# Second cross-attention of a two-layer decoder: row normalisation on ScalarE, its shift on GpSimd, statistics and aggregates as two steps, second key group turned earlier

## The chip, the cores and the metric

The kernel runs on one core of a Trainium2 chip, as a single launch that computes the whole decoder. The metric is the device time of that launch in microseconds. Before the change it is 2525.32 us, the median of 3 runs (2520.55 to 2530.87).

## The reference

A post-norm decoder of two layers on x (32 sequences of 100 rows, 256 wide) with a context of 32 times 361 rows, 256 wide. Each layer is attention, cross-attention and a feed-forward part, each followed by a layer norm of its input plus its output. The change lies in the cross-attention of the second layer, for each of the 32 sequences:

```python
q_in  = layernorm(x, gamma, beta)             # 100 x 256
kv_in = layernorm(ctx, gamma, beta)           # 361 x 256
q, k, v = q_in @ Wq.T, kv_in @ Wk.T, kv_in @ Wv.T   # 16 heads of 16
q, k = rope(q), rope(k)
attn = softmax(q @ k.T * 16 ** -0.5 + temporal_bias)
a    = (attn @ v) @ Wout.T + b_out
gate = sigmoid(a @ Wgate.T + b_gate)
out  = gate * a + (1 - gate) * x
x    = layernorm(x + out)                     # no gamma, beta
```

Everything is float32 here.

## The kernel before, in words

`decoder` calls seven stages, one behind the other: self attention, strided cross-attention, routing, experts, linear attention, `cross_attention` (the stage of this case, program names beginning with `xa_`) and the last feed-forward part (`bf_`). The linear attention (`la_`) before it also normalises rows, with ScalarE doing the product (L2145) and GpSimd computing a negated mean, the root and their product (L1939, L1944, L1947).

`cross_attention` handles one sequence ("batch" b) per period; NB is 32. Each engine runs its own program: a function `body(b, has)` is called once for each b, and `periods` calls it for all b, with a loop for the middle ones. Within one body an engine works on up to five sequences at once, at offsets -2 to +4; `later(b, 2)` is the sequence two ahead. The order of the calls in `body` is the order of the engine's instructions, written out by hand, and an engine never goes past an instruction that waits. The waits are on semaphores: `at(b, per, nth)` is the count that a semaphore has once the nth of `per` signals for b is given.

The 361 context rows of a sequence are cut into three chunks of 121 rows that share their border rows; with the 100 rows of x, padded, as a fourth lot, they fill `rows_t[121, 2, 4, 256]` (two buffers, by the parity of b). The steps for one sequence, with the engine:

1. SyncE loads the four lots (`rows`, L2492 and L2494), once the rows that were in that buffer are normalised.
2. VectorE: `moments` (four row statistics L2893, four aggregates L2898, variance plus epsilon L2902). GpSimd: `raise_power`, the power -0.5 of 121x4 numbers (L2845). VectorE: `normalise`, four times (rows - mean) * root, 121x256 each (L2909).
3. TensorE: `turn_rows`, eight transposes into the banks C1 and C2. ScalarE: `rows_out` applies gamma and beta (L2746).
4. TensorE projects keys and queries (`keys_first`, `keys_last_and_queries`) into C0 and C1. VectorE: `rope`, products with the cosine and sine tables (L2920), in two halves. GpSimd: `finish_rope`, their difference and sum (L2839, L2840).
5. TensorE: `turn_kq` for the four head groups j, each into bank C[j % 2] (L2594). ScalarE: `kq_out` copies each to `kqT` (L2786). Group 2 waits for the copy of group 0, which frees its bank, and group 3 for that of group 1.
6. TensorE: `score` for each group, 100 x 361 for four heads, into the four banks of A (L2609). VectorE: `maxima`, the row maxima of those 100 x 1444 (L2929). There is one A only: the scores, the transposed scores and their readers follow each other in it.
7. TensorE: `turn_queries` (L2621) takes the maxima along as one more column, `score_turned` for each of the three chunks computes scores the other way round, less the maxima (L2636). ScalarE: `exponential` (L2757). The product with the exponential of the bias is GpSimd's for chunks 0 and 1 (`apply_bias`, L2828) and VectorE's for chunk 2 (L2936).
8. TensorE: values (`values_first`, `values_last`), `attend` for each chunk (L2653), `turn_out`, `turn_y`, `project_out`. ScalarE copies between these (`oT` is L2752, once per sequence).
9. VectorE: `divide`, `differ` (L2954, waits for `project_out`), then ScalarE `gate` (tanh, L2780), VectorE `mix`, GpSimd `raise_power_out`, VectorE `finish` (L2975), SyncE `store`.

In TensorE's body the end runs: `values_last`, `turn_kq` 0, `score` 3, `attend` 1, `turn_kq` 1 to 3; the next body begins with `score` 0, `turn_queries`, `turn_rows`, `attend` 2, `score_turned` 0. In VectorE's: `maxima` 0, `mix`, `rope` 0, `maxima` 1, `divide`, `rope` 1, `moments`, `finish`, `maxima` 2, `normalise`, `differ`, `maxima` 3, `apply_bias`. In ScalarE's: queries, rows, `oT`, exponentials 0 and 1, values, `y_out`, exponential 2, values, `kq_out` 0, `gate`, `kq_out` 1 to 3. In GpSimd's: root of the output, bias product 0, `finish_rope`, `raise_power`, bias product 1, residual.

Of the kernel before, what the change touches and what calls it, by code (L numbers as in the profile page):

```python
# [2387 lines left out]
def cross_attention(nc, NB, x_in, x_out, w, src_len, held):  # L2388
# [9 lines left out]
    with held.ctx:  # L2398
# [42 lines left out]
        rstd = s.sb("rstd", [ROWS, LOTS])  # L2441
        power = s.sb("power", [ROWS, LOTS])
# [15 lines left out]
        stats_ready, mv_ready, var_ready, rstd_ready, normed = (s.sem(n) for n in ("stats_ready", "mv_ready", "var_ready", "rstd_ready", "normed"))  # L2458
# [21 lines left out]
        with nc.Block() as block:  # L2480
# [41 lines left out]
            def _(pe):  # L2522
# [157 lines left out]
                def body(b, has):  # L2680
# [36 lines left out]
                    if has(1):  # L2717
                        score(later(b, 1), 3, has(0))
                    if has(0):
                        attend(b, 1)  # L2720
                    if has(2):
                        for j in range(1, G):
                            turn_kq(later(b, 2), j)
# [4 lines left out]
            def _(act):  # L2728
                for sem, per in ((rowsT_ready, KC), (kqT_ready, G), (q2_ready, 1), (exp_ready, NCH), (v_ready, 2), (oT_ready, 1), (yT_ready, 1),
                                 (th_ready, 1)):  # L2730
                    act.sem_inc(sem, per * LEAD)
# [17 lines left out]
                def attended_out(b):  # L2749
                    act.wait_ge(av_done, at(b, NCH, NCH))  # L2750
                    act.wait_ge(y_turned, at(later(b, -1), 1, 1))
                    nc.scalar.activation(oT[:].rearrange("p g t -> p (g t)"), CA[:, 0:G * T], ACT.Copy).then_inc(oT_ready, 1)  # L2752

# [34 lines left out]
                def body(b, has):  # L2788
                    if has(0):
                        queries_out(b)  # L2790
                    if has(2):
                        rows_out(later(b, 2))
                    if has(-1):
                        attended_out(later(b, -1))
                    if has(0):
                        exponential(b, 0)
                        exponential(b, 1)
                    if has(1):
                        values_first(later(b, 1))
                    if has(-1):  # L2800
                        y_out(later(b, -1))
                    if has(0):
                        exponential(b, 2)
                    if has(1):
                        values_last(later(b, 1))
                    if has(2):
                        kq_out(later(b, 2), 0)
                    if has(-1):
                        gate(later(b, -1))
                    if has(2):  # L2810
                        for j in range(1, G):
                            kq_out(later(b, 2), j)

                periods(act, NB, FIRST, LAST, REACH, body)

            @block.gpsimd
            def _(pool):
                for sem, per in ((rstd_ready, 1), (summed, 1), (biased, NCH - 1), (less_ready, 1), (o_rstd_ready, 1)):
                    pool.sem_inc(sem, per * LEAD)
                nc.gpsimd.memset(power[:], -0.5).then_inc(power_set, 1)  # L2820
# [21 lines left out]
                def raise_power(b):  # L2842
                    pool.wait_ge(var_ready, at(b, 1, 1))
                    pool.wait_ge(normed, at(later(b, -1), 1, 1))
                    nc.gpsimd.tensor_tensor(rstd[:], var[:], power[:], ALU.pow).then_inc(rstd_ready, 1)  # L2845

# [12 lines left out]
                def body(b, has):  # L2859
                    if has(-2):  # L2860
                        raise_power_out(later(b, -2))
                    if has(0):
                        apply_bias(b, 0)
                    if has(2):
                        finish_rope(later(b, 2))
                    if has(3):
                        raise_power(later(b, 3))
# [9 lines left out]
            def _(dve):  # L2877
                for sem, per in ((stats_ready, 1), (mv_ready, 1), (var_ready, 1), (normed, 1), (roped, 2), (max_ready, G), (last_biased, 1),
# [10 lines left out]
                def moments(b):  # L2889
# [4 lines left out]
                    last.then_inc(stats_ready, 1)  # L2894
                    dve.wait_ge(stats_ready, at(b, 1, 1))
                    nc.vector.memset(spare[:], 0.0)
# [4 lines left out]
                    dve.wait_ge(rstd_ready, at(later(b, -1), 1, 1))  # L2901
                    nc.vector.tensor_scalar(var[:], mv[:, :, 1], LN_EPS, None, ALU.add).then_inc(var_ready, 1)  # L2902

                def normalise(b):
                    k = b[1] % 2
                    dve.wait_ge(rstd_ready, at(b, 1, 1))
                    dve.wait_ge(turned, at(later(b, -2), KC, KC))
                    for n in range(LOTS):
                        last = nc.vector.tensor_scalar(rows_n[:, k, n, :], rows_t[:, k, n, :], mv[:, n, 0:1], rstd[:, n:n + 1],  # L2909
                                                       ALU.subtract, ALU.mult)  # L2910
                    last.then_inc(normed, 1)
# [65 lines left out]
                def body(b, has):  # L2977
                    if has(1):
                        maxima(later(b, 1), 0)
                    if has(-2):  # L2980
                        mix(later(b, -2))
                    if has(2):
                        rope(later(b, 2), 0)
                    if has(1):
                        maxima(later(b, 1), 1)
                    if has(-1):
# [3 lines left out]
                    if has(3):  # L2990
                        moments(later(b, 3))
# [4 lines left out]
                    if has(3):  # L2996
                        normalise(later(b, 3))
# [7 lines left out]
                moments((0, 0))  # L3005
                dve.wait_ge(fused, 1)
# [5 lines left out]
                normalise((0, 0))  # L3012
# [567 lines left out]
```

## Time and profile before

| | |
|---|---|
| median of 3 runs | 2525.32 us (2520.55 to 2530.87) |
| the profiled execution, its own time | 2539.31 us |
| its span, first to last instruction | 2537.5 us |
| granted TensorE clock, mean of the span | 0.887 |
| TensorE busy (matmul) | 2118.6 us, 83% |
| VectorE | 1530.8 us, 60% |
| ScalarE | 950.6 us, 37% |
| GpSimd | 928.1 us, 37% |

The profile describes one execution, not the median one. Busy times are sums over the whole span, in which the seven stages follow each other; this stage fills about 1557 to 2344 us of it. PE is TensorE, PEld its weight loads, DVE VectorE, ACT ScalarE, POOL GpSimd and SP SyncE; "L2757" is a line of the kernel. In brackets behind a row of a timeline stands how long the engine was idle before it and what ended that. Busy time of TensorE is modelled and includes pipelining, so neighbouring rows overlap by some hundredths of a microsecond.

### The profile page before, as it was taken

How to read it: one execution, taken by the hardware profiler on the slowest of the kernel's cores; microseconds unless marked ns; L12 is line 12 of the kernel's file. 1: busy time of each engine (PE TensorE's matmuls, PEld its weight loads, DVE VectorE, ACT ScalarE, POOL GpSimd, SP SyncE). 2: the span in 40 equal slices, each digit the busy share in tenths (PEclk: the TensorE clock that was granted, in tenths of full speed). 3: DMA queues.
4: the chain of work that ended last, by engine and by line, in shares of the span. 5: the costliest groups of instructions: out<-in, count | busy, mean ns of one | idle time of the engine just before them, and what ended most of it. 6: DMA issues, size and time to landing. Idle time of an engine off the chain costs nothing. (4 is left out here: it accounts for less than half of the span.)

```text
span 2537.5 us, 58466 instructions
## 1 busy us (share of the span) xinstructions
PE 2118.6 (83%) x20310; PEld 1583.7 (62%) x20310; DVE 1530.8 (60%) x3550; ACT 950.6 (37%) x1881; POOL 928.1 (37%) x913
## 2 busy tenths in 40 slices
PE   6999997999776664788489996999999999996575
PEld 4666665777676554566388884666666666664233
DVE  1444443555454546233255455799999999984898
ACT  1444442333210110233134342344444444442897
POOL 0111111111134555223355431455555555553343
PEclk9999998999887786899789897899999999997555
DMA  6000003555311110877233311011110101000111
GB/s 208 30 29 29 29 25 130 207 205 212 133 48 35 34 33 23 259 222 221 73 100 90 98 44 46 21 32 31 32 32 23 32 31 32 30 13 9 52 58 46
DMA packets 157643, 192.74 MB, mean 76 GB/s; under 512 B 28517, under 2 KB 141160, under 8 KB 157559
## 3 DMA queue, kind: packets, MB, share of 16 engines
q1 hardware_dynamic: 147287, 189.03, 23.7%
q0 software_dynamic: 10272, 2.62, 0.5%
q8 instruction: 49, 0.80, 0.1%
q14 instruction: 35, 0.29, 0.0%
HBM read 140.74 MB, written 77.51 MB: 86 GB/s over the span
## 5 line engine op out<-in xcount | busy, mean ns | idle before, releaser
L2757 ACT ACTIVATE xa_prob<-xa_A 121x1600 f32<-121x1600 f32 x96 | 144.5, 1505 | 304.1 <-PE xa_A L2636 304.1
L2828 POOL TENSOR_TENSOR xa_prob<-xa_prob,xa_exp_bias 121x1600 f32<-121x1600 f32 x64 | 228.7, 3573 | 41.0 <-ACT xa_prob L2757 40.9
L2929 DVE TENSOR_REDUCE xa_kq<-xa_A 100x4 f32<-100x1444 f32 x128 | 211.6, 1653 | 21.3 <-PE xa_A L2609 21.1
L1409 POOL DMA_INDIRECT slot_rows<-rt_x_again,rt_slot_u x150 | 152.6, 1017 | 166.0 <-DVE rt_x_again L1527 103.5
L2909 DVE TENSOR_SCALAR xa_rows_n<-xa_rows_t,xa_mv,xa_rstd 121x256 f32<-121x256 f32 x128 | 142.4, 1172 | 1.1 <-POOL xa_rstd L2845 1.1
L2636 PEld LDWEIGHTS xa_A<-xa_q2T,xa_kqT 17*121 17x121 f32 x3072 | 93.9, 185 | 56.5 <-DVE xa_kq L2929 35.9
L696 DVE TENSOR_REDUCE sa_kq<-sa_A 100x16 f32<-100x1600 f32 x32 | 58.4, 1826 | 106.1 <-PE sa_A L457 106.1
L2609 PE MATMUL xa_A<-xa_kqT 16*100 16x361 f32 x1024 | 112.9, 510 | 9.9 <-ACT xa_prob L2757 6.8
L2636 PE MATMUL xa_A<-xa_q2T,xa_kqT 17*121 17x100 f32 x3072 | 109.3, 280 | 13.8 <-DVE xa_kq L2929 13.2
L1655 POOL DMA_INDIRECT contrib<-ex_y,ex_place_u x64 | 62.3, 973 | 158.5 <-ACT ex_y L1707 140.4
L2850 POOL TENSOR_TENSOR xa_o_rstd<-xa_o_var,xa_power 100x1 f32<-100x1 f32 x32 | 17.9, 560 | 252.1 <-DVE xa_o_var L2969 252.1
L1330 PEld LDWEIGHTS rt_H<-rt_xT,rt_ws 128*88 128x88 f32 x800 | 106.0, 179 | 3.7 <-issue 1.7
L654 POOL TENSOR_TENSOR sa_kq<-sa_rot_c,sa_rot_s 100x128 f32<-100x128 f32 x32 | 16.6, 519 | 247.3 <-DVE sa_rot_s L689 247.3
L2553 PE MATMUL xa_C<-xa_wk,xa_rows_T 128*121 128x256 f32 x384 | 105.4, 414 | 1.7 <-ACT xa_rows_T L2746 1.7
L1330 PE MATMUL rt_H<-rt_xT,rt_ws 128*88 128x128 f32 x800 | 106.6, 299 | 0.0
L1676 PE MATMUL ex_B<-ex_w,ex_xT 128*128 128x352 f32 x256 | 92.9, 524 | 14.8 <-issue 12.5
L1085 POOL TENSOR_TENSOR xs_rstd<-xs_var,xs_power 100x1 f32<-100x1 f32 x32 | 17.6, 550 | 232.1 <-DVE xs_var L1153 232.1
L2553 PE MATMUL xa_C<-xa_wv,xa_rows_T 128*121 128x256 f32 x384 | 101.3, 401 | 0.0
L906 PE MATMUL xs_K<-xs_ctxT,xs_wk 128*128 128x368 f32 x256 | 88.8, 490 | 10.7 <-DVE xs_y L1161 10.7
L2653 PEld LDWEIGHTS xa_CA<-xa_prob,xa_v 120*32 120x32 f32 (+1 forms) x3072 | 66.2, 111 | 43.5 <-issue 30.7
L2653 PE MATMUL xa_CA<-xa_prob,xa_v 120*32 120x100 f32 (+1 forms) x3072 | 87.8, 256 | 5.0 <-DVE xa_prob L2936 3.8
L2594 PE MATMUL xa_C<-xa_ident,xa_kq 121*128 121x121 f32 x512 | 74.1, 279 | 20.6 <-ACT xa_kqT L2786 16.3
(350 smaller groups left out, 5397.0 us busy)
## 6 DMA issues: line engine op xcount, KB each, us to landing
ex_w<-in_w13T SPq DMA_DIRECT2D x64, 352.0 KB
contrib<-xs_zero SPq DMA_DIRECT2D x30, 640.0 KB
la_rows<-contrib SPq DMA_DIRECT2D x16, 1200.0 KB
xs_ctxT<-in_ctxT SPq DMA_DIRECT2D x32, 512.0 KB
xa_rows_t<-in_ctx SPq DMA_DIRECT2D x96, 121.0 KB
ex_w<-in_w2T SPq DMA_DIRECT2D x64, 176.0 KB
slot_rows<-xs_zero SPq DMA_DIRECT2D x32, 272.0 KB
ex_x_t<-slot_rows SPq DMA_DIRECT2D x64, 136.0 KB, 2.2
```

What stands on the lines that cost most here:

```text
L906: last = nc.tensor.matmul(K[g][:, 0:NH * KPH], wk[:, c, g * P:(g + 1) * P], ctxT[:, k, c, :, 0:KPH], start=(c == 0), stop=(c == KC - 1))
L1330: last = nc.tensor.matmul(bank[:HC, m * P:(m + 1) * P], ws[:, c, m * HC:(m + 1) * HC], xT[:, k, c, :], start=(c == 0), stop=(c == KC - 1))
L1409: nc.gpsimd.indirect_dma_start(slot_rows, bass.IndirectOffsetOnAxis(slot_u[:, k, n:n + 1], 0), x_again[:, k, :], None, bounds_check=SLOTS ...
L1676: last = nc.tensor.matmul(B[u][:, 0:2 * FE], xT[:, u, c, :], w13[:, u, c], start=(c == 0), stop=(c == KC - 1))
L2553: last = nc.tensor.matmul(bank[:ROWS, o:o + D], rows_T[:, k, c, a:a + ROWS], wm[:, c, :], start=(c == 0), stop=(c == KC - 1))
L2609: last = nc.tensor.matmul(A[:T, h, 0:src_len], kqT[rows, k, j, src_len:src_len + T], kqT[rows, k, j, 0:src_len], start=True, stop=True)
L2636: last = nc.tensor.matmul(A[:ROWS, h, j * T:(j + 1) * T], kqT[rows, k, j, n * STEP:n * STEP + ROWS], q2T[rows, j, :], start=True, stop=True)
L2653: last = nc.tensor.matmul(CA[32 * h:32 * h + 32, j * T:(j + 1) * T], v1[0:rows, k, n, 4 * j + h, :], prob[0:rows, n, o:o + T], start=(n == ...
L2757: nc.scalar.activation(prob[:, n, :].rearrange("p (h a) -> p h a", h=HPG), A[:ROWS, :, 0:G * T], ACT.Exp, scale=EXP_SCALE).then_inc(exp_re ...
L2828: nc.gpsimd.tensor_tensor(chunk, chunk, exp_bias[:, n, :].unsqueeze(1).to_broadcast([ROWS, HEADS, T]), ALU.mult).then_inc(biased, 1)
L2909: last = nc.vector.tensor_scalar(rows_n[:, k, n, :], rows_t[:, k, n, :], mv[:, n, 0:1], rstd[:, n:n + 1], ALU.subtract, ALU.mult)
L2929: nc.vector.tensor_reduce(kq[:T, k, NCH, 4 * j:4 * j + 4, DH:DH + 1].rearrange("p h o -> p (h o)"), A[:T, :, 0:src_len], axis=AXIS_X, op=A ...
```

## The change

The normalisation of the rows moves from VectorE to ScalarE, as root * row + shift, an activation with a scale and a bias from tiles; the shift, minus mean times root, is made by GpSimd with two small operations around the root (`nmean`, `shift`; `nothing` holds zeros). `moments` is split: the row statistics stand before `rope` 0 in VectorE's body, and `aggregate` stands between `maxima` 1 and `divide`. `raise_power` stands before `finish_rope` in GpSimd's body. `normalise` stands between `y_out` and exponential 2 in ScalarE's. `turn_kq` 1 stands before `attend` 1 in TensorE's.

```diff
--- before.py
+++ after.py
@@ -2439,6 +2439,9 @@
         mv = s.sb("mv", [ROWS, LOTS, 2])
         var = s.sb("var", [ROWS, LOTS])
         rstd = s.sb("rstd", [ROWS, LOTS])
+        nmean = s.sb("nmean", [ROWS, LOTS])
+        shift = s.sb("shift", [ROWS, LOTS])
+        nothing = s.sb("nothing", [ROWS, LOTS])
         power = s.sb("power", [ROWS, LOTS])
         o_stats = s.sb("o_stats", [T, 6])
         o_mv = s.sb("o_mv", [T, 2])
@@ -2455,7 +2458,8 @@
         loaded = [s.sem(f"loaded{k}") for k in range(2)]
         res_loaded = [s.sem(f"res_loaded{k}") for k in range(2)]
         stored = [s.sem(f"stored{k}") for k in range(2)]
-        stats_ready, mv_ready, var_ready, rstd_ready, normed = (s.sem(n) for n in ("stats_ready", "mv_ready", "var_ready", "rstd_ready", "normed"))
+        stats_ready, mv_ready, var_ready, rstd_ready, shift_ready, normed = (s.sem(n) for n in (
+            "stats_ready", "mv_ready", "var_ready", "rstd_ready", "shift_ready", "normed"))
         turned, rowsT_ready = s.sem("turned"), s.sem("rowsT_ready")
         projected, roped, summed = s.sem("projected"), s.sem("roped"), s.sem("summed")
         kq_turned, kqT_ready = s.sem("kq_turned"), s.sem("kqT_ready")
@@ -2716,10 +2720,12 @@
                         turn_kq(later(b, 2), 0)
                     if has(1):
                         score(later(b, 1), 3, has(0))
+                    if has(2):
+                        turn_kq(later(b, 2), 1)
                     if has(0):
                         attend(b, 1)
                     if has(2):
-                        for j in range(1, G):
+                        for j in range(2, G):
                             turn_kq(later(b, 2), j)
 
                 periods(pe, NB, FIRST, LAST, REACH, body)
@@ -2727,7 +2733,7 @@
             @block.scalar
             def _(act):
                 for sem, per in ((rowsT_ready, KC), (kqT_ready, G), (q2_ready, 1), (exp_ready, NCH), (v_ready, 2), (oT_ready, 1), (yT_ready, 1),
-                                 (th_ready, 1)):
+                                 (th_ready, 1), (normed, 1)):
                     act.sem_inc(sem, per * LEAD)
                 act.wait_ge(w_in, W_ALL)
                 act.wait_ge(cleared, 2)
@@ -2750,6 +2756,15 @@
                     act.wait_ge(av_done, at(b, NCH, NCH))
                     act.wait_ge(y_turned, at(later(b, -1), 1, 1))
                     nc.scalar.activation(oT[:].rearrange("p g t -> p (g t)"), CA[:, 0:G * T], ACT.Copy).then_inc(oT_ready, 1)
+
+                def normalise(b):
+                    k = b[1] % 2
+                    act.wait_ge(shift_ready, at(b, 1, 1))
+                    act.wait_ge(turned, at(later(b, -2), KC, KC))
+                    for n in range(LOTS):
+                        last = nc.scalar.activation(rows_n[:, k, n, :], rows_t[:, k, n, :], ACT.Identity, scale=rstd[:, n:n + 1],
+                                                    bias=shift[:, n:n + 1])
+                    last.then_inc(normed, 1)
 
                 def exponential(b, n):
                     act.wait_ge(shifted, at(b, NCH, n + 1))
@@ -2799,6 +2814,8 @@
                         values_first(later(b, 1))
                     if has(-1):
                         y_out(later(b, -1))
+                    if has(3):
+                        normalise(later(b, 3))
                     if has(0):
                         exponential(b, 2)
                     if has(1):
@@ -2811,12 +2828,14 @@
                         for j in range(1, G):
                             kq_out(later(b, 2), j)
 
+                normalise((0, 0))
                 periods(act, NB, FIRST, LAST, REACH, body)
 
             @block.gpsimd
             def _(pool):
-                for sem, per in ((rstd_ready, 1), (summed, 1), (biased, NCH - 1), (less_ready, 1), (o_rstd_ready, 1)):
+                for sem, per in ((rstd_ready, 1), (shift_ready, 1), (summed, 1), (biased, NCH - 1), (less_ready, 1), (o_rstd_ready, 1)):
                     pool.sem_inc(sem, per * LEAD)
+                nc.gpsimd.memset(nothing[:], 0.0)
                 nc.gpsimd.memset(power[:], -0.5).then_inc(power_set, 1)
                 nc.gpsimd.memset(v1[:], 1.0).then_inc(v_set, 1)
                 pool.wait_ge(power_set, 1)
@@ -2842,7 +2861,10 @@
                 def raise_power(b):
                     pool.wait_ge(var_ready, at(b, 1, 1))
                     pool.wait_ge(normed, at(later(b, -1), 1, 1))
+                    nc.gpsimd.tensor_tensor(nmean[:], nothing[:], mv[:, :, 0], ALU.subtract)
                     nc.gpsimd.tensor_tensor(rstd[:], var[:], power[:], ALU.pow).then_inc(rstd_ready, 1)
+                    pool.wait_ge(rstd_ready, at(b, 1, 1))
+                    nc.gpsimd.tensor_tensor(shift[:], nmean[:], rstd[:], ALU.mult).then_inc(shift_ready, 1)
 
                 def raise_power_out(b):
                     pool.wait_ge(o_var_ready, at(b, 1, 1))
@@ -2861,10 +2883,10 @@
                         raise_power_out(later(b, -2))
                     if has(0):
                         apply_bias(b, 0)
+                    if has(3):
+                        raise_power(later(b, 3))
                     if has(2):
                         finish_rope(later(b, 2))
-                    if has(3):
-                        raise_power(later(b, 3))
                     if has(0):
                         apply_bias(b, 1)
                         residual(b)
@@ -2875,7 +2897,7 @@
 
             @block.vector
             def _(dve):
-                for sem, per in ((stats_ready, 1), (mv_ready, 1), (var_ready, 1), (normed, 1), (roped, 2), (max_ready, G), (last_biased, 1),
+                for sem, per in ((stats_ready, 1), (mv_ready, 1), (var_ready, 1), (roped, 2), (max_ready, G), (last_biased, 1),
                                  (rec_ready, 1), (y_ready, 1), (dg_ready, 1), (dif_ready, 1), (r_ready, 1), (o_stats_ready, 1),
                                  (o_mv_ready, 1), (o_var_ready, 1), (out_ready, 1)):
                     dve.sem_inc(sem, per * LEAD)
@@ -2892,23 +2914,16 @@
                     for n in range(LOTS):
                         last = nc.vector.bn_stats(stats[:, n, :], rows_t[:, k, n, :])
                     last.then_inc(stats_ready, 1)
+
+                def aggregate(b):
                     dve.wait_ge(stats_ready, at(b, 1, 1))
+                    dve.wait_ge(shift_ready, at(later(b, -1), 1, 1))
                     nc.vector.memset(spare[:], 0.0)
                     for n in range(LOTS):
                         last = nc.vector.bn_aggr(mv[:, n, :], stats[:, n, :])
                     last.then_inc(mv_ready, 1)
                     dve.wait_ge(mv_ready, at(b, 1, 1))
-                    dve.wait_ge(rstd_ready, at(later(b, -1), 1, 1))
                     nc.vector.tensor_scalar(var[:], mv[:, :, 1], LN_EPS, None, ALU.add).then_inc(var_ready, 1)
-
-                def normalise(b):
-                    k = b[1] % 2
-                    dve.wait_ge(rstd_ready, at(b, 1, 1))
-                    dve.wait_ge(turned, at(later(b, -2), KC, KC))
-                    for n in range(LOTS):
-                        last = nc.vector.tensor_scalar(rows_n[:, k, n, :], rows_t[:, k, n, :], mv[:, n, 0:1], rstd[:, n:n + 1],
-                                                       ALU.subtract, ALU.mult)
-                    last.then_inc(normed, 1)
 
                 def rope(b, half):
                     dve.wait_ge(projected, at(b, 2, half + 1))
@@ -2979,22 +2994,22 @@
                         maxima(later(b, 1), 0)
                     if has(-2):
                         mix(later(b, -2))
+                    if has(3):
+                        moments(later(b, 3))
                     if has(2):
                         rope(later(b, 2), 0)
                     if has(1):
                         maxima(later(b, 1), 1)
+                    if has(3):
+                        aggregate(later(b, 3))
                     if has(-1):
                         divide(later(b, -1))
                     if has(2):
                         rope(later(b, 2), 1)
-                    if has(3):
-                        moments(later(b, 3))
                     if has(-2):
                         finish(later(b, -2))
                     if has(1):
                         maxima(later(b, 1), 2)
-                    if has(3):
-                        normalise(later(b, 3))
                     if has(-1):
                         differ(later(b, -1))
                     if has(1):
@@ -3003,13 +3018,13 @@
                         apply_bias(b)
 
                 moments((0, 0))
+                aggregate((0, 0))
                 dve.wait_ge(fused, 1)
                 for i in range(KC):
                     nc.vector.tensor_copy(wog[:, i, D:2 * D], C[i][:, 0:D])
                 for k in range(2):
                     last = nc.vector.tensor_tensor(less[:, k, D:2 * D], C[2][:T, 0:D], bg[:], ALU.add)
                 last.then_inc(fused_sb, 1)
-                normalise((0, 0))
                 periods(dve, NB, FIRST, LAST, REACH, body)
 
 ROUND = 12582912.0
```

## Rows read from the trace of the kernel before

**Rows 1.** Windows, steady stretch: us; busy PE, PEld, DVE, ACT, POOL; clock, DMA, GB/s.
```profile
1630.87:2267.89 637.02, 605.56 (x8120) 419.81 (x8120) 582.69 (x918) 285.50 (x422) 352.55 (x223) 1.00 0.09 28
```

**Rows 2.** One line's instructions in the same stretch: line L2752.
```profile
L2752 ACT ACTIVATE xa_oT<-xa_CA x29: 501/502/507, 1630.9 to 2267.9; 128x400 f32<-128x400 f32 x29
```

**Rows 3.** Waits of TensorE, same stretch: us in total, times, longest.
```profile
PE xa_C L2594 <- ACT xa_kqT L2786: 15.5, 28, 0.6
PE xa_A L2636 <- DVE xa_kq L2929: 9.3, 28, 0.4
PE xa_A L2609 <- ACT xa_prob L2757: 4.5, 28, 0.2
```

**Rows 4.** Timeline of one period (start us, us, instructions): TensorE.
```profile
1919.40 0.87 PE L2609 MATMUL xa_A<-xa_kqT 16*100 16x361 f32 x8 [0.15 <-ACT xa_prob L2757]
...
1920.20 0.89 PE L2653 MATMUL xa_CA<-xa_prob,xa_v 120*32 120x100 f32 x32
...
1921.02 1.05 PE L2594 MATMUL xa_C<-xa_ident,xa_kq 121*128 121x121 f32 x8
...
1922.62 0.63 PE L2594 MATMUL xa_C<-xa_ident,xa_kq 121*128 121x121 f32 x4 [0.56 <-ACT xa_kqT L2786]
...
1923.29 0.87 PE L2609 MATMUL xa_A<-xa_kqT 16*100 16x361 f32 x8
...
1924.08 0.56 PE L2621 MATMUL xa_C<-xa_ident,xa_kq 100*128 100x100 f32 x4
...
1924.48 0.99 PE L2546 MATMUL xa_C<-xa_ident,xa_rows_n 121*128 121x121 f32 x8
...
1925.40 0.89 PE L2653 MATMUL xa_CA<-xa_prob,xa_v 121*32 121x100 f32 x32
...
1926.68 1.10 PE L2636 MATMUL xa_A<-xa_q2T,xa_kqT 17*121 17x100 f32 x32 [0.38 <-DVE xa_kq L2929]
```

**Rows 5.** The same timeline: VectorE.
```profile
1916.30 4.76 DVE L2909 TENSOR_SCALAR xa_rows_n<-xa_rows_t,xa_mv,xa_rstd 121x256 f32<-121x256 f32 x4
...
1920.98 0.68 DVE L2954 TENSOR_TENSOR xa_dg<-xa_C,xa_less 100x512 f32<-100x512 f32 x1
...
1921.59 1.65 DVE L2929 TENSOR_REDUCE xa_kq<-xa_A 100x4 f32<-100x1444 f32 x1
...
1923.15 1.81 DVE L2936 TENSOR_TENSOR xa_prob<-xa_prob,xa_exp_bias 121x1600 f32<-121x1600 f32 x1
...
1924.89 1.65 DVE L2929 TENSOR_REDUCE xa_kq<-xa_A 100x4 f32<-100x1444 f32 x1
...
1929.83 0.69 DVE L2920 TENSOR_TENSOR xa_k_c<-xa_C,xa_cos 121x512 f32<-121x512 f32 x1 [1.54 <-PE xa_C L2553]
...
1934.42 1.39 DVE L2893 BATCH_NORM_STATS2 xa_stats<-xa_rows_t 121x6 f32<-121x256 f32 x4
```

**Rows 6.** The same timeline: ScalarE.
```profile
1917.84 1.51 ACT L2757 ACTIVATE xa_prob<-xa_A 121x1600 f32<-121x1600 f32 x1 [3.92 <-PE xa_A L2636]
...
1921.69 0.42 ACT L2780 ACTIVATE xa_th<-xa_dg 100x256 f32<-100x256 f32 x1 [1.61 <-DVE xa_dg L2954]
```

**Rows 7.** The same timeline: GpSimd.
```profile
1934.75 1.27 POOL L2839 TENSOR_TENSOR xa_kq<-xa_k_c,xa_k_s 121x512 f32<-121x512 f32 x1 [1.66 <-DVE xa_k_s L2920]
...
1937.43 1.04 POOL L2845 TENSOR_TENSOR xa_rstd<-xa_var,xa_power 121x4 f32<-121x4 f32 x1 [0.18 <-DVE xa_var L2902]
```

**Rows 8.** Timeline of the stage's start: VectorE.
```profile
1566.22 1.38 DVE L2909 TENSOR_SCALAR xa_rows_n<-xa_rows_t,xa_mv,xa_rstd 121x256 f32<-121x256 f32 x4
```

**Rows 9.** Groups by line, linear attention (1300 to 1550 us).
```profile
L2145 ACT ACTIVATE la_x_o<-la_r,la_shift,la_rstd 100x256 f32<-100x256 f32 x30 | 16.2, 588 | 1.5 <-POOL la_shift L1947 1.5
...
L1939 POOL TENSOR_TENSOR la_nmean<-la_mv,la_minus 100x4 f32<-100x4 f32 (+1 forms) x17 | 3.4, 199 | 132.9 <-DVE la_var L2249 132.9
```

**Rows 10.** Timeline near the stage's end: VectorE.
```profile
2275.74 0.40 DVE L2975 TENSOR_SCALAR xa_x_o<-xa_r,xa_o_mv,xa_o_rstd 100x256 f32<-100x256 f32 x1
```

**Rows 11.** Windows: a stretch of the linear attention, columns as in rows 1.
```profile
1395.00:1400.00 5.00, 5.00 (x26) 5.00 (x26) 1.92 (x12) 0.59 (x2) 3.07 (x4) 0.50 0.58 167
```

## The prediction

> **What bounds the kernel now.** I read five views in this order. First the windows of the changed stage between two steady points [rows 1]: 637.02 us in which TensorE is busy 605.56, that is 95%, at a granted clock of 1.00, with VectorE at 582.69 (91%), ScalarE at 285.50 and GpSimd at 352.55. [Rows 2] says how many batches that is: 29 copies of `oT`, so 28 periods of 637.02 / 28 = 22.75 us. TensorE is the bound and has 31.5 us of idle time in it; the edit can only win that idle time and what each restart of a stalled matmul stream costs. Then the waits of TensorE in the same stretch [rows 3]: 15.5 us (28 times) for ScalarE's copy of a transposed key group, 9.3 us (28 times) for VectorE's row maxima, 4.5 us (28 times) for the exponential. They add up to 29.3 of the 31.5 us. Last the timelines of one period, engine by engine [rows 4 to 7], which say why those waits are there.
>
> The end of a period on TensorE [rows 4]: score group 3 starts at 1919.40, attend 1 at 1920.20, the transposes of key groups 1 and 2 at 1921.02, group 3 only at 1922.62 behind an idle 0.56, score 0 of the next batch at 1923.29, the query turn at 1924.08, the row turn at 1924.48, attend 2 at 1925.40, and the first transposed score at 1926.68 behind an idle 0.38. Two causes, and one of them lies on VectorE [rows 5]. Its four normalisations start at 1916.30 and take 4.76 us; the same four took 1.38 us when GpSimd was quiet at the start of the stage [rows 8]. Only behind them comes `differ` (1920.98), then maxima 3 (1921.59), although its scores started at 1919.40 and take 0.87, then the bias product (1923.15), then maxima 0 (1924.89 + 1.65 = 1926.54), which the first transposed score waits for. And `differ` being late, ScalarE's tanh waits 1.61 us for it [rows 6], with the copies of key groups 1 to 3 queued behind it, so the two PSUM banks in which keys are turned come free late.
>
> **The change part by part.** *Normalisation off VectorE.* Removed from its queue: 4.76 us per period [rows 5]. `differ` then has only the output projection to wait for and comes ahead of score 3, so tanh no longer waits, and maxima 3 can start when its scores end. *Key group 1 turned before attend 1:* its copy runs beside attend 1 (0.89), and the copies of groups 1 and 2 no longer form a chain with the turns.
>
> The sum, on TensorE, from the starts of [rows 4], for the stretch from score 3 to the first transposed score: score 3 0.80, one turn 0.50 (half of the pair's 1.05, less the overlap), attend 1 0.82, two turns 1.00, score 0 0.79, query turn 0.40, row turn 0.92, attend 2 0.87 (its 0.89 less overlap). Together 6.10 us against 1926.68 - 1919.40 = 7.28 now: 1.18 us less per period. It is more than the 0.56 + 0.38 of idle, since a turn that stands alone holds the stream 0.67 (1922.62 to 1923.29) and not 0.50.
>
> What is late next: VectorE's chain over the same stretch. Maxima 3 starts 0.92 behind score 3 (its 0.87 and a hand-over of 0.05), and by the distances of [rows 5] the bias product 1.56 later and maxima 0 1.74 later, ending at 0.92 + 1.56 + 1.74 + 1.65 = 5.87; with 0.14 to TensorE (1926.54 to 1926.68) 6.01. TensorE arrives at 6.10: a tie, and I keep 0.13 us per period back for it. So 1.05 us per period, 28 x 1.05 = 29.4 us. From both sides: at least the two waits of [rows 3] in part, 24.8 us if they go whole; at most 28 x 1.18 = 33 us. The exponential's 4.5 us stays.
>
> *Statistics before the first rope product.* Their 1.39 us [rows 5] (the row at 1934.42) go to a place where VectorE is idle 1.54 us behind the mix (the row at 1929.83): they fit with 0.15 to spare, cost nothing. If that cover were gone, rope 0, maxima 1 and the second transposed score would be late by what sticks out. *Aggregates before the division.* 0.5 us of aggregates and the small add, here beside GpSimd's wait and not beside its product, push division and second rope product back by 0.65 us. The y turn and GpSimd's rope wait for these; the latter sits idle 1.66 us for the rope now [rows 7].
>
> *GpSimd.* Added: one subtract and one multiply on a few elements; the subtract of the linear attention took 199 ns [rows 9], and I take the same for the multiply. The root takes 1.04 [rows 7]. The aggregates are ready behind maxima 1, some 1.3 us before GpSimd's rope would start; 0.2 + 1.04 + 0.2 and the waits between are about 1.7 us. The rope's start moves from 1934.75 to some 1935.4 (the later of this and the late second rope product), but the root no longer stands between rope and the second bias product: the bias starts 0.5 us earlier than now. Between 0.4 us lost and 0.5 won per period on an engine busy 55%; I take nothing, since no wait of TensorE in [rows 3] names GpSimd.
>
> *ScalarE.* Added: four activations with scale and bias from a tile. The trace has the form at 100 partitions, 588 ns [rows 9], so 2.35 us. They stand before exponential 2, where ScalarE is idle 3.92 us [rows 6]. Covered with 1.5 us to spare, if the shift is there by then. From rope 0 at 1929.83 [rows 5]: two rope products and maxima 1, 3.0; aggregates 0.6; GpSimd 1.7; the shift is ready at 1935.1. The latest point is the next exponential 2 less the four, 1917.84 + 22.75 - 2.35 = 1938.2. Without cover each microsecond goes straight onto the score chain.
>
> *The queue of SyncE.* Rows are reloaded behind `normed`, now some 5 us earlier, and the statistics read them 6 us earlier, a whole period behind; no wait on a load shows in [rows 3], so nothing.
>
> *Start and end.* In the first batch the four normalisations lie open: 2.35 us on ScalarE instead of 1.38 [rows 8], with 0.4 for the small operations: +1.4 us, once.
>
> Sum: -29.4 + 1.4 = -28 us. The profiled execution took 2539.31 us (span 2537.5 and 1.8 around it), so 2511.3 by its own time; the median of the runs is 2525.32, 14 us below it, so 2497.3 us there. I forecast 2497.
>
> **The rivals.** *A, only the idle time in part goes (chance 0.18).* The tie above falls the other way, or `finish`, now straight behind the second rope product, runs into GpSimd's rope. Its price: in the bad case it waits for both of GpSimd's rope products, 2 x 1.27 us [rows 7], maxima 2 and the third transposed score slip by about 0.65 us per period, 28 x 0.65 = 18 us, leaving -10: 2515. For it: the stretched 4.76 of [rows 5] against 1.38. Against it: where the same order occurs in the trace, near the end without statistics between, `finish` took 0.40 [rows 10], since it starts before GpSimd is released. The Trainium skill ("GPSIMD Engine Reference", Key points) says that GpSimd shares its SBUF interfaces with VectorE and contends with instructions in a 2-port mode or with two SBUF inputs. By that rule the bias product on VectorE would be at risk too, once it moves forward by a microsecond; the trace has the stretched normalisation (4.76 us), and [rows 10] shows no price for `finish`.
>
> *B, the edit does not do what it says (chance 0.08).* The turns still wait, because what frees the banks is ScalarE's queue, which has 2.35 us more to do. Then only the maxima's wait goes, 9.3 us [rows 3], less 1.4 at the start: -8, 2517. Against it: the copy of group 0 and tanh would be done before turn 1 ends.
>
> *C, slower: the clock (chance 0.05).* Place: the steady stretch. The trace has a stretch in which TensorE was busy 5.00 of 5 us at a granted clock of 0.50, which is 1.2 GHz and not 2.4 [rows 11], in the linear attention; so busy time alone doesn't keep the clock up. Such a stretch costs 2.5 us. One in each period would be 70 us: 2497 + 70 = 2567. It makes the kernel slower by a measurable amount from (28 + 12.6) / 2.5 = 16 stretches on. Against it: the same instructions run at 1.00 for 637 us [rows 1]. The Trainium skill ("TensorE: Matmul & The Clock Gate", Part 1) holds the reverse, that the throttled state is the default and activity releases it. By that rule denser work keeps 1.00, and the sum stands; [rows 11] speaks against taking busy time as that activity.
>
> **How the numbers follow.** The forecast has 0.69, A 0.18, B 0.08, C 0.05. Its own range is the 24.8 to 33 us of above, with the start: 2493 to 2502. For 8 in 10 I take 2489 to 2516: below, restarts that cost more than rows show; above, as far as A. A measurement of this kernel tells about 0.5%, 12.6 us, from no change, so faster is below 2512.7: nearly all of the forecast and a third of A and B together, 0.77; same 0.18; slower 0.05.
>
> **What would show it.** Right: a period of 21.6 to 21.8 us between copies of `oT`; no wait of the group turns for ScalarE above 0.1 us; the wait for the maxima near zero; VectorE's busy time per period down by about 5 us (the 4.76 first); ScalarE's idle time before exponential 2 at about 1.6 us; TensorE busy above 98%. Wrong: `finish` longer than 1 us (A), tanh or key copies still waited for (B), a clock below 1.00 in the steady stretch (C), or the first transposed score still behind maxima 0 by 0.3 us.

## The result and the profile after

The changed kernel took 2500.57 us (median of 4 runs, 2497.24 to 2503.42) beside 2528.1 us for the kernel before (4 runs, 2520.55 to 2539.12): a ratio of 0.9878 with a 95% interval of 0.9847 to 0.9909. It is faster, by 27.5 us or 1.2%; 2497 was forecast. On another occasion it was 2506.66 (6 runs) beside 2534.38 (11 runs), ratio 0.9882 (0.9842 to 0.9921), 27.7 us less. A ratio here and below is the time over that of the kernel before on the same chip, with its 95% interval.

The steady stretch of the changed stage, in the columns of [rows 1], and the copies of `oT` in it, as in [rows 2]:

```profile
1626.26:2230.49 604.23, 599.77 (x8128) 418.66 (x8127) 436.50 (x806) 339.79 (x534) 357.56 (x279) 1.00 0.10 30
```

```profile
L2758 ACT ACTIVATE xa_oT<-xa_CA x29: 500/502/504, 1626.3 to 2230.5; 128x400 f32<-128x400 f32 x29
```

Again 28 periods, of 604.23 / 28 = 21.58 us where there were 22.75: 32.8 us less. TensorE is busy 599.77 of 604.23 us, 99.3%, VectorE 5.2 us less per period, and the clock is 1.00 as before. Of TensorE's three waits [rows 3] one is left, and it has not changed:

```profile
PE xa_A L2613 <- ACT xa_prob L2772: 4.5, 28, 0.2
```

The timeline of a period's end on TensorE, from score 3 to the first transposed score, against [rows 4]:

```profile
1900.47 0.87 PE L2613 MATMUL xa_A<-xa_kqT 16*100 16x361 f32 x8 [0.15 <-ACT xa_prob L2772]
...
1901.27 0.63 PE L2598 MATMUL xa_C<-xa_ident,xa_kq 121*128 121x121 f32 x4
...
1901.84 0.89 PE L2657 MATMUL xa_CA<-xa_prob,xa_v 120*32 120x100 f32 x32
...
1902.66 1.05 PE L2598 MATMUL xa_C<-xa_ident,xa_kq 121*128 121x121 f32 x8
...
1903.64 0.87 PE L2613 MATMUL xa_A<-xa_kqT 16*100 16x361 f32 x8
...
1905.76 0.89 PE L2657 MATMUL xa_CA<-xa_prob,xa_v 121*32 121x100 f32 x32
...
1906.58 1.10 PE L2640 MATMUL xa_A<-xa_q2T,xa_kqT 17*121 17x100 f32 x32
```

1906.58 - 1900.47 = 6.11 us, where it was 7.28. Group 1 is turned at 1901.27, groups 2 and 3 as a pair at 1902.66 with nothing idle before them. VectorE in the same period, against [rows 5]:

```profile
1886.41 1.41 DVE L2915 BATCH_NORM_STATS2 xa_stats<-xa_rows_t 121x6 f32<-121x256 f32 x4
...
1888.07 0.69 DVE L2935 TENSOR_TENSOR xa_k_c<-xa_C,xa_cos 121x512 f32<-121x512 f32 x1 [0.26 <-PE xa_C L2557]
...
1891.33 0.17 DVE L2926 TENSOR_SCALAR xa_var<-xa_mv 121x4 f32<-121x4 f32 x1
...
1893.23 0.40 DVE L2990 TENSOR_SCALAR xa_x_o<-xa_r,xa_o_mv,xa_o_rstd 100x256 f32<-100x256 f32 x1
...
1897.86 0.69 DVE L2969 TENSOR_TENSOR xa_dg<-xa_C,xa_less 100x512 f32<-100x512 f32 x1 [1.02 <-PE xa_C L2681]
...
1901.41 1.67 DVE L2944 TENSOR_REDUCE xa_kq<-xa_A 100x4 f32<-100x1444 f32 x1 [2.86 <-PE xa_A L2613]
...
1902.99 1.81 DVE L2951 TENSOR_TENSOR xa_prob<-xa_prob,xa_exp_bias 121x1600 f32<-121x1600 f32 x1
...
1904.72 1.66 DVE L2944 TENSOR_REDUCE xa_kq<-xa_A 100x4 f32<-100x1444 f32 x1
```

The statistics (1886.41) fill the gap behind the mix, and rope 0 still waits 0.26 us for TensorE. The variance (1891.33) takes 0.17 us, `finish` (1893.23) 0.40, `differ` (1897.86) waits for nothing but the projection, and maxima 3 (1901.41) starts as its scores end. ScalarE and GpSimd, against [rows 6, 7]:

```profile
1894.88 2.06 ACT L2765 ACTIVATE xa_rows_n<-xa_rows_t,xa_shift,xa_rstd 121x256 f32<-121x256 f32 x4
...
1898.92 1.50 ACT L2772 ACTIVATE xa_prob<-xa_A 121x1600 f32<-121x1600 f32 x1 [1.97 <-PE xa_A L2640]
...
1901.03 0.43 ACT L2795 ACTIVATE xa_th<-xa_dg 100x256 f32<-100x256 f32 x1
```

```profile
1891.58 0.20 POOL L2864 TENSOR_TENSOR xa_nmean<-xa_nothing,xa_mv 121x4 f32<-121x4 f32 x1 [0.25 <-DVE xa_var L2926]
...
1891.73 1.01 POOL L2865 TENSOR_TENSOR xa_rstd<-xa_var,xa_power 121x4 f32<-121x4 f32 x1
...
1892.82 0.20 POOL L2867 TENSOR_TENSOR xa_shift<-xa_nmean,xa_rstd 121x4 f32<-121x4 f32 x1
...
1893.55 1.26 POOL L2858 TENSOR_TENSOR xa_kq<-xa_k_c,xa_k_s 121x512 f32<-121x512 f32 x1 [0.53 <-DVE xa_k_s L2935]
...
1896.01 3.58 POOL L2847 TENSOR_TENSOR xa_prob<-xa_prob,xa_exp_bias 121x1600 f32<-121x1600 f32 x1
```

The shift is ready at 1893.02, the four activations run from 1894.88 in 2.06 us, and 1.97 us of idle time are left before exponential 2. Tanh (1901.03) has no idle time before it.

Outside the 28 periods the stage differs by 2.7 us. Up to its first `oT` it took 73.5 us before and 70.4 after, from the last of the 29 to the stage's end 75.7 and 76.1.

### The profile page after: what moved, and what is told of

Its sections match the earlier page's. It is cut to its first block and busy times, and to the rows that moved or that the text cites. A ratio compares the mean times of both kernels' runs of the same rounds, so it can differ in the third digit from the quotient of the medians.

```text
span 2501.3 us, 58541 instructions
## 1 busy us (share of the span) xinstructions
PE 2103.3 (84%) x20307; PEld 1575.3 (63%) x20310; DVE 1374.4 (55%) x3422; ACT 1012.0 (40%) x2009; POOL 934.4 (37%) x978
## 5 line engine op out<-in xcount | busy, mean ns | idle before, releaser
L1676 PEld LDWEIGHTS ex_B<-ex_w,ex_xT 128*128 128x128 f32 x256 | 56.6, 227 | 52.1 <-issue 21.1
L1387 ACT ACTIVATE rt_th<-rt_H 88x512 f32<-88x512 f32 x25 | 14.8, 592 | 182.0 <-DMA x<-sa_x_o 119.9
L2801 ACT ACTIVATE xa_kqT<-xa_C 128x482 f32<-128x482 f32 x128 | 70.1, 573 | 44.0 <-PE xa_C L2598 44.0
```

The source lines that it names most:

```text
L1676: last = nc.tensor.matmul(B[u][:, 0:2 * FE], xT[:, u, c, :], w13[:, u, c], start=(c == 0), stop=(c == KC - 1))
L2801: nc.scalar.activation(kqT[:, k, j, :], C[j % 2][:, 0:WIDE], ACT.Copy).then_inc(kqT_ready, 1)
```

## The experiments

Periods below are the distance of the first and the 29th copy of `oT`, divided by 28, in the profile of each kernel. The two profiles of the changed kernel, from different occasions, agree to a hundredth of a microsecond (21.58), while its total times spread over 24 us, so the periods carry the verdicts. Single periods within one profile differ by up to 0.15 us, in the kernel before by up to 0.46. e1 to e4 ran on a chip on which the kernel before took 2395.49 us (19 runs). It was not profiled there; that its period is 22.75 there too is taken from e1, whose profile has the same period and whose total time is the same as that of the kernel before.

### e1: the second key group earlier, alone

```diff
 (kernel before, TensorE)
+turn_kq(later(b, 2), 1)
 attend(b, 1)
-for j in range(1, G): turn_kq(later(b, 2), j)
+for j in range(2, G): turn_kq(later(b, 2), j)
```

> The kernel before, with the second key group turned ahead of attend 1 and nothing else. Theory: alone it is worth nothing, because ScalarE still has tanh ahead of the copy of group 1, and tanh waits for VectorE behind its long normalisation; that copy ends at the same moment and group 3 waits for it as before. Period 22.65 to 22.75 us (22.75 before), total within 3 us of before. Rival, the order of the turns is worth its own half: the 0.56 us wait of the group turns goes, period 22.1 to 22.2, total 16 to 18 us less.

Period 22.75 us, total 2390.17 (ratio 1.0006, 0.9974 to 1.0037). Nothing, as the theory said; the interval excludes the rival's 16 to 18 us. TensorE's waits, and the rows around the turn of group 3:

```profile
PE xa_C L2594 <- ACT xa_kqT L2788: 11.2, 27, 0.4
PE xa_A L2636 <- DVE xa_kq L2931: 9.3, 28, 0.4
PE xa_A L2609 <- ACT xa_prob L2759: 4.5, 28, 0.2
```

```profile
1768.45 0.68 DVE L2956 TENSOR_TENSOR xa_dg<-xa_C,xa_less 100x512 f32<-100x512 f32 x1
...
1769.16 0.42 ACT L2782 ACTIVATE xa_th<-xa_dg 100x256 f32<-100x256 f32 x1 [1.62 <-DVE xa_dg L2956]
...
1769.48 1.02 ACT L2788 ACTIVATE xa_kqT<-xa_C 128x482 f32<-128x482 f32 x2
...
1770.09 0.63 PE L2594 MATMUL xa_C<-xa_ident,xa_kq 121*128 121x121 f32 x4 [0.42 <-ACT xa_kqT L2788]
```

`differ` comes at 1768.45, tanh waits 1.62 us for it and the copies of groups 1 and 2 start at 1769.48. The idle time before group 3 is shorter (11.2 us against 15.5), but only because group 2 is turned later; group 3 starts at the same point of the period, 3.24 us behind score 3 (1766.85 to 1770.09) and 3.22 before.

### e2: the changed kernel without that move

```diff
 (changed kernel, TensorE)
-turn_kq 1 | attend 1 | turn_kq 2, 3
+attend 1 | turn_kq 1, 2, 3
```

> The changed kernel with the second key group turned behind attend 1 again. Theory: with tanh early, what is left of the wait is the chain turn 1, copy 1, turn 3: 0.25 us idle and a restart of 0.1 to 0.15; period 21.9 to 22.0 against 21.58, total some 10 us more than the changed kernel. Rival, the waits were tanh's alone: period 21.6, no difference.

Period 21.90, total 2358.42 (ratio 0.9869, 0.9833 to 0.9904, against a kernel before of 22.75 per period).

```profile
PE xa_C L2598 <- ACT xa_kqT L2799: 6.9, 28, 0.2
PE xa_A L2613 <- ACT xa_prob L2770: 4.4, 28, 0.2
```

6.9 us of idle time, 0.25 per turn, and 0.07 of restart: the move is worth 0.32 us per period with the rest of the change, 9 us, and nothing without it. The total does not show these 9 us: its ratio is no higher than the changed kernel's 0.9882, and the two intervals overlap. The start of the stage, which also enters the total, took 68.0 us to the first `oT` here and 70.4 and 67.7 in the changed kernel's two profiles.

### e3: statistics, aggregates and root at their old places

```diff
 (changed kernel, VectorE and GpSimd)
-mix | moments | rope 0 | maxima 1 | aggregate | divide | rope 1
+mix | rope 0 | maxima 1 | divide | rope 1 | moments | aggregate
-raise_power | finish_rope
+finish_rope | raise_power
```

> The changed kernel with statistics, aggregates and root at their old places in VectorE's and GpSimd's order. Theory: the shift is ready some 4 us later, at about 1.9 us before exponential 2 could start, and the four activations need 2.06: exponential 2 is late by 0.1 to 0.2 us, period 21.6 to 21.8, total 0 to 6 us more than the changed kernel. Rival, the split carries much of the gain: period 22.0 or more, total over 12 us more.

Period 21.89, total 2369.58 (ratio 0.9905, 0.9875 to 0.9935). Between the two expectations: 0.31 us per period, 9 us.

```profile
PE xa_A L2613 <- ACT xa_prob L2772: 13.2, 28, 0.7
```

```profile
1763.99 0.99 DVE L2926 TENSOR_SCALAR xa_var<-xa_mv 121x4 f32<-121x4 f32 x1
...
1766.41 0.20 POOL L2867 TENSOR_TENSOR xa_shift<-xa_nmean,xa_rstd 121x4 f32<-121x4 f32 x1
...
1766.65 2.08 ACT L2765 ACTIVATE xa_rows_n<-xa_rows_t,xa_shift,xa_rstd 121x256 f32<-121x256 f32 x4 [2.23 <-POOL xa_shift L2867]
...
1768.63 1.48 ACT L2772 ACTIVATE xa_prob<-xa_A 121x1600 f32<-121x1600 f32 x1
```

The variance takes 0.99 us beside GpSimd's rope, where the changed kernel has 0.17, the shift ends at 1766.61, and exponential 2 follows the fourth activation instead of the scores. The start of the stage is longer too: 79.7 us to the first `oT`, 68.0 in e2. ScalarE's copies of the first keys stand behind a normalisation that waits for late statistics, and start 27.3 us into the stage instead of 24.5. That is 2.8 of the 11.7 us; over the whole of the start the granted clock was also lower, 0.74 against 0.85, and what the rest is due to was not isolated.

### e4: every move, but the normalisation stays on VectorE

```diff
 (kernel before)
+turn_kq 1 before attend 1; moments before rope 0;
+aggregate before divide; raise_power before finish_rope
 (normalise as before: VectorE, behind maxima 2)
```

> All moves of the change (second key group, statistics, aggregates, root), but the normalisation stays on VectorE behind maxima 2. Theory: it still waits for GpSimd's second bias product, which starts about 0.5 us earlier, so differ and tanh come only some 0.4 us earlier: period 22.2 to 22.5. Rival, the reordering and not the engine is the gain: period below 21.8.

Period 23.13, slower than before by 0.38 us, 11 us in the steady stretch; total 2398.62 (ratio 1.0036, 1.0008 to 1.0064). Both expectations missed.

```profile
PE xa_C L2594 <- ACT xa_kqT L2788: 21.8, 28, 0.8
```

```profile
1768.63 4.41 POOL L2830 TENSOR_TENSOR xa_prob<-xa_prob,xa_exp_bias 121x1600 f32<-121x1600 f32 x1
...
1769.39 5.77 DVE L2913 TENSOR_SCALAR xa_rows_n<-xa_rows_t,xa_mv,xa_rstd 121x256 f32<-121x256 f32 x4
...
1773.01 0.91 POOL L2858 TENSOR_TENSOR xa_less<-xa_bo,xa_x_res 100x256 f32<-100x256 f32 x1
```

The normalisation (1769.39) takes 5.77 us here and not 4.76, and GpSimd's product beside it (1768.63) 4.41 and not 3.58; the residual starts at 1773.01. In all 28 periods the first of the four ends 0.15 us behind the product, as in the kernel before (below, e8), but the product is itself longer (4.28 to 4.56 us). So moving the parts changed what the meeting costs. What sets that was not found.

### e8: GpSimd's second bias product cut to one head

```diff
 (kernel before, GpSimd, apply_bias)
-chunk of HEADS heads
+chunk of HEADS heads for n == 0, of one head for n == 1
```

> The kernel before, where GpSimd's second bias product takes one head of sixteen only (the other fifteen are left out, so their probabilities lack the bias in that chunk). Theory, VectorE's normalisation waits for GpSimd's instruction: the four take 1.4 to 1.8 us and not 4.76, differ and tanh are early, and the period falls to 21.9 to 22.1. Rival, the four are slow by themselves with these operands in the steady stretch: 4.76 stays, period 22.75.

First what the meeting looks like in the kernel before. The first of the four normalisations starts inside GpSimd's product and ends 0.15 us behind it, in all 28 periods:

```profile
1915.66 3.58 POOL L2828 TENSOR_TENSOR xa_prob<-xa_prob,xa_exp_bias 121x1600 f32<-121x1600 f32 x1
...
1916.30 3.08 DVE L2909 TENSOR_SCALAR xa_rows_n<-xa_rows_t,xa_mv,xa_rstd 121x256 f32<-121x256 f32 x1
```

With the product cut the period is 21.90; one run, 2515.26 beside 2527.84 us. The four normalisations of a period:

```profile
L2910 DVE TENSOR_SCALAR xa_rows_n<-xa_rows_t,xa_mv,xa_rstd 121x256 f32<-121x256 f32 x112 | 39.3, 411 | 0.0
```

39.3 us for 112 of them, 1.4 us for four, where [rows 5] has 4.76. This kernel has the normalisation on VectorE, the old order of the turns and old statistics, and its period is that of e2 (21.90). So the operation is not slow; in the kernel before it waits for GpSimd's. The meeting has not gone, though, it is paid by the other engine. The same rows in one period of e8:

```profile
1905.18 2.24 POOL L2857 TENSOR_TENSOR xa_less<-xa_bo,xa_x_res 100x256 f32<-100x256 f32 x1
...
1905.47 1.37 DVE L2910 TENSOR_SCALAR xa_rows_n<-xa_rows_t,xa_mv,xa_rstd 121x256 f32<-121x256 f32 x4
```

GpSimd's residual, which now meets the four, takes 2.24 us where it took 0.78 before. It costs nothing, since no wait of TensorE names GpSimd, here as in [rows 3].

### e5 and e6: a doubled load on ScalarE, half a microsecond more on VectorE

```diff
 (changed kernel, ScalarE, normalise)
+four more activations into a tile that nothing reads
 (changed kernel, VectorE, behind apply_bias)
+nc.vector.memset(idle[:], 0.0)    # 100 x 512
```

> The changed kernel, where ScalarE makes each of the four normalisations twice (once into a tile that nothing reads). Theory: ScalarE is idle 1.97 us before exponential 2, and 2.06 us more is 0.1 us too much: period 21.6 to 21.75. Rival, the normalisation on ScalarE is already on the path: period near 23.6, the full 2.06 more.

> The changed kernel with one fill of a 100x512 tile on VectorE behind its bias product, about 0.3 to 0.5 us. Theory: maxima 3, bias product, maxima 0 is the next bound with 0.06 us of slack, so the period grows by the fill less 0.06: 21.85 to 22.05. Rival, TensorE alone is the bound and VectorE has slack: period 21.58.

e5: period 21.58, no change and so just under what was expected; one run, 2511.78 us. The eight end just as exponential 2 could start:

```profile
1908.66 2.07 ACT L2769 ACTIVATE xa_rows_n<-xa_rows_t,xa_shift,xa_rstd 121x256 f32<-121x256 f32 x4
...
1910.73 1.50 ACT L2776 ACTIVATE xa_prob<-xa_A 121x1600 f32<-121x1600 f32 x1
```

e6: period 22.01; one run, 2521.76 us. The fill takes

```profile
L2954 DVE MEMSET xa_idle<- 100x512 f32 x28 | 13.6, 485 | 1.6
```

and the period grew by 0.43 of its 0.485: the chain from maxima 3 to maxima 0 has 0.06 us of slack and no more. On ScalarE the four added activations push the others back by 1.97 us (from 1906.69 to 1908.66), which is all of the idle time it had.

### e7, e10 and e11: the last wait

e9 is the changed kernel once more, for the ratio above:

> The changed kernel again, in more rounds on another occasion. Theory: the stage's share is 28 x 1.17 = 33 us of the steady stretch plus about 0 to 3 us at its start, so the ratio is 0.986 to 0.988. Rival, part of the profile's 36 us is chance in other stages: the ratio is nearer 0.989, and the stage alone is still 33 to 36 us shorter.

Period 21.58 again; the ratio came out at 0.9882, between the two expectations, and its interval holds both.

```diff
 e7 (changed kernel, TensorE)
-score 3 | turn_kq 1 | attend 1
+attend 1, first head group | score 3 | turn_kq 1 | attend 1, other three
 e10 (changed kernel)
-chunk 2's bias product on VectorE
+apply_bias(b, 2) on GpSimd, behind apply_bias(b, 1)
 e11: both
```

> The changed kernel with the first head group's quarter of attend 1 (8 products, 0.2 us) ahead of score 3, the rest behind. Theory: it fills the 0.15 us wait for exponential 2, and the maxima start 0.05 us later, which the chain on VectorE just bears: period 21.42 to 21.5, total 2 to 4.5 us less than the changed kernel. Rival, the chain on VectorE is the bound already: period 21.58 to 21.65.

> The changed kernel with the bias product of chunk 2 on GpSimd, attend 1 whole. Theory: TensorE is the bound of the changed kernel and the chain on VectorE only ties with it, so freeing VectorE by 1.81 us does nothing: period 21.57 to 21.59. Rival, the chain on VectorE binds: period 21.5 or less.

> The split of attend 1 as before, and the bias product of chunk 2 made by GpSimd instead of VectorE, behind its second product. Theory: the split gave nothing only because maxima 3, bias product, maxima 0 ended with TensorE; without the product in that chain maxima 0 has 0.3 us of slack, and the period falls to TensorE's own work, 21.43 to 21.52, total 2 to 4 us less than the changed kernel. Rival, the split costs TensorE its own restarts, 0.15 us: period 21.58 to 21.65 as with the split alone. GpSimd's product ends some 1.5 us before attend 2 needs it; if it is late, the period is above 21.7.

e7: period 21.60, total 2502.69 (ratio 0.9856, 0.9821 to 0.9891; that is no difference from e9). The rival's period came. The wait for the exponential is filled with work, and another came, unnamed in the waits but plain in the starts:

```profile
1924.97 0.87 PE L2613 MATMUL xa_A<-xa_kqT 16*100 16x361 f32 x8
...
1929.21 1.66 DVE L2947 TENSOR_REDUCE xa_kq<-xa_A 100x4 f32<-100x1444 f32 x1
...
1930.08 0.89 PE L2657 MATMUL xa_CA<-xa_prob,xa_v 121*32 121x100 f32 x32
...
1931.02 1.10 PE L2640 MATMUL xa_A<-xa_q2T,xa_kqT 17*121 17x100 f32 x32
```

Maxima 0 ends at 1930.87, and the first transposed score starts 0.94 us behind attend 2 and not 0.82. e10: period 21.58, as the theory said, one run (2368.54 beside 2388.92 us). e11: period 21.49, inside its theory's range, total 2361.48 beside 2388.92 (ratio 0.9866, 0.9796 to 0.9937), with

```profile
1491.17:2092.81 601.64, 601.64 (x8128) 418.20 (x8127) 390.41 (x778) 339.79 (x534) 457.84 (x307) 1.00 0.10 30
```

TensorE busy 601.64 of 601.64 us. e11 beats both kernels in the stretch, by 2.6 us over the change, which no total time here can tell.

## Why the prediction was right, step by step

**The bound and the two causes.** Right. TensorE had 31.5 us of idle time and has 4.5 left. That the late maxima and the late tanh have one origin, the stretched normalisation, is shown by e8, which shortens GpSimd's product and with it the normalisation, leaves everything else, and gets 0.85 of the 1.17 us per period. That it is stretched by GpSimd is shown by the same kernel.

**The two parts of the edit work only together.** The prediction took both into one sum and did not price them apart. Apart they are: the turn alone 0 (e1), everything but the turn 0.85 us per period (e2), both 1.17. The engine move is the substance; without it the rest costs 0.38 us (e4).

**The sum of 6.10 us.** Measured 6.11, by two errors that cancel: the lone turn was put at 0.50, although the prediction itself had seen one hold the stream for 0.67, and took 0.57 (1901.27 to 1901.84); attend 2 was put at 0.87 and took 0.82. The mis-sized term is the 0.13 us held back for the tie with VectorE: the chain ended 0.06 us ahead of TensorE (e6), and nothing of the reserve was used. The steady stretch gave 32.8 us and not 29.4, and the period of 21.58 lies just below the 21.6 to 21.8 named as the sign of being right.

**Statistics at no cost.** Right that they cost nothing: rope 0 waits for TensorE as before. But the step was priced for what it costs and not for what it is worth: late statistics would have made exponential 2 late by 0.31 us per period (e3).

**GpSimd.** Right: 0.20 + 1.01 + 0.20 us; the rope starts 0.24 us after its last input (1893.31 to 1893.55), and the second bias product directly behind it. Counted from the first transposed score the rope starts 0.5 us later than before and the product 0.75 earlier; 0.65 and 0.5 were forecast. **ScalarE.** Right: 2.06 us for four against 2.35 forecast, 1.97 us of cover left against 1.5, shown by e5.

**The start.** Forecast +1.4 us. The first row turn starts 1.5 us later, counted from the stage's first instruction (11.8 against 10.3 us), as forecast. But the stage reaches its first `oT` 3.1 us earlier, which the prediction did not foresee. The place is the stretch of the first transposed scores, where the granted clock (third value from the end) is lower before than after. Before, and then after, the 9 us from 1603 to 1612:

```profile
1603.00:1612.00 9.00, 9.00 (x61) 6.58 (x60) 1.67 (x1) 4.08 (x5) 1.18 (x1) 0.50 0.17 54
```

```profile
1603.00:1612.00 9.00, 8.22 (x92) 5.74 (x92) 6.34 (x15) 3.77 (x5) 3.56 (x1) 1.00 0.04 14
```

This is not one profile's chance alone: to the first `oT` the kernels with the normalisation on VectorE, e8 among them, took 72.8 to 73.7 us (4 profiles), the changed one and those close to it 67.7 to 70.9 (7 profiles), e5 73.5 and e3 79.7. But the size is partly chance: the two profiles of the changed kernel differ by 2.7 us (70.4 and 67.7), nearly as much as before and after, and their mean granted clock up to there was 0.79 and 0.85, where the kernel before had 0.74. What brings the full clock forward was not isolated.

**The total.** -28 forecast, -27.5 and -27.7 measured. The absolute 2497 was 3.6 us too low, since the kernel before came out at 2528.10 us with its fourth run and not at 2525.32. The stretch (-32.8) and the start (-3.1) sum to more, and so did the pair of profiles (2539.31 to 2503.17, -36). The interval of the ratio, 23 to 39 us of 2528, holds all of these, so the totals cannot tell them apart. That the total came out at 28 is luck in its last digits: it does not confirm the 0.13 us reserve or the +1.4 us at the start, and the periods and the start refute them.

**The rivals.** A fell: `finish` took 0.40 us in all 27 cases, and the maxima's wait is gone. The bias product on VectorE, which the text on A held to be at risk, took 1.81 us as before; GpSimd had ended its residual 2.15 us ahead of it (1900.84 to 1902.99), so the two do not meet and the runs do not test it. B fell as a whole, though e1 shows that ScalarE's queue is what it would have hung on. C fell: the clock is 1.00 in the stretch at 99.3% busy.

## What to carry to other kernels

Before pricing a move, measure how long the same instruction takes where its neighbour engine is quiet; 1.38 against 4.76 us was most of this case, 0.85 of 1.17 us per period (e8). When two waits follow each other in a loop, sum the starts along each engine over the same stretch and compare them: 6.10 and 6.01 told how much the edit could give, and what would be late next. An edit worth nothing alone can be worth a quarter of the gain behind another one, so test the parts from both sides, alone and left out.

## What the runs showed of the hardware

In the kernel before, a row operation of VectorE from SBUF to SBUF with pointer scalars (121x256, 0.40 us by itself) that started 0.64 us into a product of GpSimd lasted 3.08 us, until 0.15 us behind the end of that product; a 121x4 one took up to 0.99 us and not 0.17. It is not always VectorE that waits: in e8 the four normalisations started 0.29 us into GpSimd's residual and took 1.37 us together, and the residual 2.24 instead of 0.78. In e4 both were longer, 5.77 us for 4.76 and 4.41 for 3.58. What decides who waits was not found. VectorE's statistics (1.39 to 1.41 us) and its maxima from PSUM (1.65 to 1.67) were the same beside GpSimd's work and without it, and so were the four activations of ScalarE (2.06 us, and 2.07 in the first batch).

From the start of four transposes that stand alone to the start of the next group TensorE took 0.57 us, with eight in a row half of 0.98.
